# Who takes the rounding constant off: GpSimd for two tiles of four in the ternary stage of a two-layer decoder

## The reference

```python
def act_quant(x):
    scale = 127.0 / jnp.clip(jnp.max(jnp.abs(x), axis=-1, keepdims=True), 1e-05)
    return jnp.clip(jnp.round(x * scale), -128, 127) / scale

def bit_linear(x, w):            # weight_quant(w): round(w / mean|w|), cut to -1, 0, 1, times mean|w|
    xq = x + jax.lax.stop_gradient(act_quant(x) - x)
    wq = w + jax.lax.stop_gradient(weight_quant(w) - w)
    return jnp.einsum('bsd,hd->bsh', xq, wq)

h = bit_linear(x, w1)                            # 256 -> 1024
h = depthwise_conv1d(h.transpose(0, 2, 1), conv_w, conv_b)
h = jax.nn.silu(h.transpose(0, 2, 1))
return bit_linear(h, w2)                         # 1024 -> 256
```

## Time and profile before

| | before |
|---|---|
| median of 3 runs | 2252.4 us (2250.98 to 2253.33) |
| the profiled execution's own time | 2255.41 us |
| its span in the trace | 2253.6 us |
| TensorE busy | 2005.1 us, 89% |
| DVE busy | 1743.7 us, 77% |
| ACT busy | 1344.6 us, 60% |
| GpSimd busy | 206.5 us, 9% |
| rounded i (line 1823) | 16 times, median 684 ns |

### The profile page before, as it was taken

How to read it: one execution, slowest core, us unless ns; L and a number is a source line. 1 busy time by engine, 2 the same in 40 slices (tenths; PEclk the granted TensorE clock), 3 DMA queues, 4 the chain that set the end, 5 groups by cost and what they waited for, 6 DMA issues and landing times.

```text
span 2253.6 us, 43048 instructions
## 1 busy us (share of the span) xinstructions
PE 2005.1 (89%) x17990; PEld 1135.5 (50%) x17990; DVE 1743.7 (77%) x2680; ACT 1344.6 (60%) x1997; POOL 206.5 (9%) x215
## 2 busy tenths in 40 slices
PE   2899978888989997989999998898998999888988
PEld 1576653423656774242466666433255677533225
DVE  7787878695878877789588887869767788786956
ACT  3566656487356655738536664565844666465772
POOL 2000001140000000015000000101400000011310
PEclk9999999999999999999999999899999999999999
DMA  6176730020046670001006766001001677400100
GB/s 259 37 126 115 130 64 1 1 81 25 19 78 120 123 132 19 2 18 77 11 20 112 127 116 117 1 2 76 21 10 39 117 125 127 83 1 1 76 2 10
DMA packets 417314, 147.67 MB, mean 66 GB/s; under 512 B 404440, under 2 KB 412768, under 8 KB 416224
## 3 DMA queue, kind: packets, MB, share of 16 engines
q1 hardware_dynamic: 416544, 142.82, 31.0%
q0 software_dynamic: 576, 2.10, 0.3%
HBM read 41.86 MB, written 2.10 MB: 20 GB/s over the span
## 4 chain that ended last, share of the span: by engine, by line
PE 54%; DVE 25%; DMA 8%; ACT 6%; issue 5%; POOL 1%; SPq 0%; POOLq 0%; DVEq 0%; ACTq 0%
DVE nmx L1856 10%; PE ps L581 10%; PE ps L583 10%; PE ps L582 10%; DMA arena<-arena 6%; PE ps L931 4%; PE ps L743 3%; PE ps L973 2%; PE ps L917 2%; DVE arena L1666 2%; PE ps L737 2%; PE ps L738 2%; PE ps L885 1%; PE ps L601 1%; DVE st L1494 1%
## 5 line engine op out<-in xcount | busy, mean ns | idle before, releaser
L1856 DVE TENSOR_REDUCE nmx<-ps 128x2 f32<-128x1024 f32 x384 | 444.1, 1219 | 21.1 <-PE ps L885 19.3
L1371 ACT ACTIVATE arena<-ps 128x512 f32<-128x512 f32 x768 | 405.2, 602 | 52.9 <-PE ps L917 47.7
L581 PE MATMUL ps<-arena 128*128 128x512 f16 (+1 forms) x800 | 273.9, 342 | 3.8 <-DVE arena L1997 2.7
L582 PE MATMUL ps<-arena 128*128 128x512 f16 (+1 forms) x800 | 273.4, 342 | 0.0
L583 PE MATMUL ps<-arena 128*128 128x512 f16 (+1 forms) x800 | 273.3, 342 | 0.0
L1653 DVE TENSOR_SCALAR_CACHE_REDUCE ps<-ps 128x1536 f32<-128x1536 f32 x128 | 225.8, 1764 | 46.7 <-PE ps L583 46.1
L931 PE MATMUL ps<-arena 128*17 128x256 f32 x3072 | 237.4, 385 | 0.0
L1666 DVE SCALAR_TENSOR_TENSOR arena<-arena,rs 128x1536 f16<-128x1536 f32 x128 | 231.6, 1810 | 4.2 <-ACT arena L1265 4.2
L1265 ACT ACTIVATE arena<-arena,rs 128x1536 f16<-128x1536 f32 x128 | 200.8, 1568 | 40.1 <-DVE rs L1659 40.1
L1258 ACT ACTIVATE arena<-ps,nm 128x1536 f32<-128x1536 f32 x128 | 197.1, 1540 | 11.7 <-DVE ps L1653 11.7
L737 PE MATMUL ps<-arena 128*128 128x128 f16 x1536 | 185.3, 219 | 2.4 <-DMA arena<-arena 2.4
(11 more groups left out here) (259 smaller groups left out, 3850.0 us busy)
## 6 DMA issues: line engine op xcount, KB each, us to landing
arena<-in_experts SPq DMA_DIRECT2D x4, 3840.0 KB, 11.7
arena<-in_weights SPq DMA_DIRECT2D x8, 929.0 KB, 12.6
arena<-in_ctx SPq DMA_DIRECT2D x4, 1024.0 KB, 6.2
arena<-arena SPq DMA_TRANSPOSE x256, 3.7
arena<-in_ctx_t SPq DMA_DIRECT2D x4, 1024.0 KB, 4.9
arena<-in_ternary SPq DMA_DIRECT2D x2, 1024.0 KB, 5.8
y<-in_x POOLq DMA_DIRECT2D x4, 512.0 KB, 4.2
x<-in_x SPq DMA_DIRECT2D x4, 512.0 KB, 3.8
```

The lines of the kernel that those rows point to most:

```text
L581: mm(out_, lh, rh, start=(k == 0), stop=False)
L582: mm(out_, lh, rl_, start=False, stop=False)
L1371: A(pr_[:, n % RING, :], ps[:, 4 + n % 3, :], ACT.Exp).then_inc(b_exp.sem, 1)
L1856: V.tensor_reduce(nmx[:, g_ % 2, ch, :, pp, i], ps[:, 2 * (z % 2):2 * (z % 2) + 2, :], AX.X, ALU.max, negate=True)\
```

## The change

Three things are different. GpSimd gets a function `first_quantise`, which takes the constant off tiles 0 and 1, behind its two inverse roots for the norm of this stage and ahead of the one for the next stage. It counts a new semaphore, `g_first`. DVE keeps only rounded 2 and rounded 3, which it does behind max 3, so the four maxima with their scales follow each other. TensorE waits on `g_first` for T0 and T1 and on `g_quant` for T2 and T3. ACT waits in addition on `g_first` before it overwrites a buffer of `gt` with scaled 2 and scaled 3. Names: `gi` and `gt` lie in `arena`.

```diff
-        g_t, g_quant, gq_t, gq_done = sig("g_t", NT), sig("g_quant", NT), sig("gq_t", NT), sig("gq_done", NT)
+        g_t, g_quant, gq_t, gq_done = sig("g_t", NT), sig("g_quant", 2), sig("gq_t", NT), sig("gq_done", NT)
+        g_first = sig("g_first", 2)
...
+            def first_quantise(b):
+
+                for i in range(2):
+                    pool.wait_ge(g_scaled.sem, g_scaled.at(b, i + 1))
+                    nc.gpsimd.tensor_scalar(gi[:, i, :], gt[:, i, :], ROUND, None, ALU.subtract).then_inc(g_first.sem, 1)
...
+                    if k == 1:
+                        first_quantise(b)
...
-                        pe.wait_ge(g_quant.sem, g_quant.at(b, j + 1))
+                        rounded, n = (g_first, j + 1) if j < 2 else (g_quant, j - 1)
+                        pe.wait_ge(rounded.sem, rounded.at(b, n))
...
                     act.wait_ge(g_scale.sem, g_scale.at(b, i + 1))
+                    if i >= 2:
+                        act.wait_ge(g_first.sem, g_first.at(b, i - 1))
...
                     dve.wait_ge(g_scaled.sem, g_scaled.at(b, i + 1))
-                    if i >= 2:
-                        dve.wait_ge(gq_t.sem, gq_t.at(b, i - 1))
+                    dve.wait_ge(gq_t.sem, gq_t.at(b, i - 1))
...
-                ivs = [row_scales(0), row_scales(1)]
-                for i in range(2, NT):
-                    quantise(i - 2)
-                    ivs.append(row_scales(i))
+                ivs = [row_scales(i) for i in range(NT)]
                 quantise(NT - 2)
                 add_tile(0, ivs[0])
                 quantise(NT - 1)
```

## The result

The changed kernel takes 2264.23 us, the median of six runs (2257.57 to 2268.84), against 2253.27 (2250.98 to 2254.89) for the kernel before on the same chips: a ratio of 1.0035, 95% interval 1.0019 to 1.0052. In a second set it was 2260.89 against 2251.42, ratio 1.0044 (1.0028 to 1.0060). It is 8 to 10 us slower by the ratios, where 2.1 us less were forecast, and both medians lie above the high end of the range, 2256.4.

A forecast was written before the change was run, and what follows sets the result against it. T1's start on TensorE, waiting for rounded 1 behind max 2 on DVE, was taken to bound the stage. 0.52 us a batch over four batches gives -2.1 us, 2252.4 to 2250.3; range 2246.5 to 2256.4.

The forecast's parts named there:

- the high end of the range: Slowest forecast median, 2256.4 us, with GpSimd's subtraction at 2.12 us and T1 0.99 us later per batch.
- What bounds the stage: T1's start on TensorE sets the rest; it waits for rounded 1, held 1.02 us behind max 2 on DVE.
- the length X: Duration of each subtraction moved to GpSimd: between 1.04 and 2.12 us, taken as 1.1; break-even at 1.62.
- The place and the sum: T1 starts 1.62 - X earlier, 0.52 us a batch, so 2.1 us less over four batches.
- Is anything else late: Copy 1, scaled 3, T2 and T3 hold nothing up; TensorE's whole row moves 0.52 us earlier.
- Rival 1: GpSimd's subtraction costs 2.12 us like the two-input one; T1 0.99 us later, 4.0 us lost, 2256.4; chance 0.15.
- Rival 2: GpSimd shuts out DVE's small scale operations: 2.5 to 3.2 us lost, 2263 with X = 2.12 as well; chance 0.08.
- The clock: TensorE's clock in the stretches from scaled 0 to add 3: put at zero, between 2.5 us saved and 2.3 lost.

The follow-up runs named there:

- The cast: Changed kernel with GpSimd casting tiles 0 and 1 to fp16 instead of subtracting, their rounding left out: 2248.15 us against 2251.42 for the kernel before, ratio 0.9980.
- tile 1 alone: Kernel before with only tile 1's subtraction moved to GpSimd, tile 0's staying on DVE: 2261.68 us against 2251.42, ratio 1.0038.

## Why the prediction was wrong, step by step

**What bounds the stage: right.** T1's start sets the rest. T1 stood at 2.89, 3.90, 4.46, 4.60, 5.75 and 6.87 us in six kernels, and the four stretches then measured 45.0, 48.9, 51.0, 52.2, 55.7 and 58.3 to 61.5 us.

**"Moved to GpSimd", the length X: wrong, and this is the step that failed.** The prediction said "X lies between 1.04 and 2.12 us. I take 1.1, near the cast, since both read one tensor and write one". X is 2.77 us, outside both ends. The two nearest rows were taken as bounds, and they bounded the number of inputs, not the operation. The runs show that an operation with a constant costs 2.5 ns a column and is dearer than one with a second tensor: 2.77 us, four times DVE's 0.684. The rule of the Trainium skill ("GPSIMD Engine Reference", engine selection) that was weighed beside it, one-input operations at roughly line rate, holds roughly here for copy and cast (1.04) and not for an operation with a constant (2.8). Its other half sets GpSimd against DVE, where the prediction compared two rows of GpSimd; against DVE's own addition of two tensors of 128x1024 (line 1583, 1.22 us) GpSimd's 2.12 is 1.7 times as long, near that half.

**The place and the sum hold with the right X; that the total fits as well is in part luck.** Above 1.62 the prediction's own sum is rounded 0 and rounded 1 in a row: T1 at 1.21 + 0.08 + 2 x 2.77 + 0.06 = 6.89 us; measured 6.87. 4 x (6.87 - 4.60) = 9.1 us, which gives 2252.4 + 9.1 = 2261.5, inside both measured intervals (4 to 12 and 6 to 14 us over the kernel before). The cast shows the same from the other side: with X = 1.04 the kernel gains. But the stretches of the two profiles grew by 6.1 and 9.3 us, not by 9.1 each time, and about half of the loss goes with a lower clock over the whole program (below), which this sum does not hold.

**"Is anything else late": right for the dear case too.** Rounded 2 and scaled 2 slip with GpSimd, and T2 follows product 0 as before.

**Rival 1 was the one that came true, with too low an end.** It priced X at 2.12 and 4.0 us; it had the mechanism, the place and the sign. A chance of 0.15 for it and 2256.4 as the high end were both too small because X was closed above.

**Rival 2: not seen.** DVE's one-column operations took 153 to 154 ns beside GpSimd's instruction, as they did before (line 1770, 153 to 155):

```profile
L1782 DVE TENSOR_SCALAR quant<-quant x16: 153/154/154, 326.2 to 1975.8; 128x1 f32<-128x1 f32 x16
```

**The clock: the place was too narrow.** I looked at it inside the stretch only. TensorE is also idle for 1.8 us between product 3 and the next stage, and in 24 of 40 batches the clock falls soon after TensorE starts again (ten profiled executions without matmuls added there). Over those 40 batches `self_attention` takes 79.2 to 79.5 us where it does not fall, 80.3 to 80.4 where it falls, and 80.7 to 82.1 where it falls once more some 30 us later. The run with matmuls in both gaps shows that idleness there brings it on: with the gap filled the stage takes 79.2 to 79.4 us in place of 79.4 to 81.1.

The granted clocks of the single executions tell what one profile could not. Over the 76 executions of the kernel before in the experiments, the time is 1.2 us longer for each 0.001 that the mean granted clock is lower (a fitted line). In the set of the second measurement that mean is 0.985 for the kernel before, 0.981 for the changed kernel and 0.979 for tile 1 alone. By this line, an estimate, 4 to 5 of the changed kernel's 10 us and 6 to 7 of the tile 1 version's 9.5 (means) go with the clock, the part of it inside the stretch included. So what the tile 1 version lost beyond its T1 appears to lie there. Why a later T1 lowers the clock outside the stretch is not shown.

## What to carry to other kernels

The nearest rows of a trace bound a new instruction's cost only if they run the same operation; where none does, leave the upper end open, here by as much again, and look at what the sum does there. Before giving an instruction to an idle engine, ask for the duration at which it breaks even (here 1.62 us against 0.68 on DVE) and how sure one is to stay below. And look for a way to have the work done by instructions that are there already: ACT's write to fp16 can round and its next copy can subtract, which took 1.7 us a batch off T1's start. In the kernel's time that gain showed only when TensorE's idle gap behind product 3 was filled.

## What the runs showed of the hardware

- GpSimd, 128x1024 from float32: copy or cast 1.04 us, subtraction of a second tensor 2.12 to 2.36, subtraction of or multiplication by a constant 2.77 to 2.86 (the subtraction 1.49 at 512 columns).
- A DVE subtraction from SBUF to SBUF, begun while GpSimd ran such an operation, took 1.21 to 1.26 us, not 0.68, and did not wait for GpSimd's end. GpSimd's own time did not change. One-column operations of DVE were not slowed (0.15 us).
- An fp16 write by ACT of x + 1536 rounds x well enough to replace the float32 constant and the subtraction in this stage; copy i with a bias took 1.10 to 1.14 us against 1.02 without.
- The 10 us behind a gap of 1.8 us on TensorE had a granted clock of 0.83 in 24 of 40 batches and 1.00 in the other 16 (ten profiled executions); with 1.5 us of unread matmuls in the gap it was 1.00 in 12 of 12.
